# One wait fewer per pair: the gather's half-way wait for the gram, kept in the first block of each pair only

## The chip, the cores and the metric

The kernel runs on 1 core of one Trainium2 chip. The metric is the device time of one execution in microseconds (us); lower is better.

## What is computed

Two residual layers on x of shape 8 x 256 x 128 x 128 (8 images, 256 channels), all in float32. Layer 0 is a modulated deformable sampling; layer 1 is a group whitening whose matrix needs the second moments of the whole result of layer 0.

```
# layer 0
n   = group_norm(x, 32)
off = conv3x3(n, offset_w) + offset_b          # 4 groups, dx and dy
mod = 1 + tanh(conv3x3(n, mod_w) + mod_b)
v   = conv1x1(n, kv_w)[C:] + kv_b              # 8 heads of 32 channels
s   = bilinear sample of v at (pixel + off), times mod
x1  = x + conv1x1(s, out_w) + out_b
# layer 1
n   = group_norm(x1, 32)
cov = per 16 channels, mean over all images and pixels of (n - mu)(n - mu)^T, + 1e-4 I
out = x1 + cov^(-1/2) (n - mu) * weight + bias
```

## The kernel before, in words

Every image has 128 rows of pixels. A **block** is 4 rows (512 pixels) and a **pair** is two blocks, j = 0 and j = 1; an image has 16 pairs, i = 0 to 15. The images run through a software pipeline: while image g is sampled (bilinear sums, output convolution, residual, gram), image a = g + 1 goes through its convolution and its places and weights are computed, and image a + 1 is read for its norm statistics. The last image is sampled with no other image's convolution beside it. Each engine has an instruction list of its own, in an order written out by hand, and the engines meet on semaphores only.

One block of the sampled image takes these steps.

- **GpSimd** (`gather`, L1021): 16 indirect DMAs (L1034), NJ = 16, each fetching 128 patches of 256 floats from the stored `v2` into `patch[n]`. Four patch buffers stand in a ring (RING = 4), n = 2 * (i mod 2) + j. Before its first DMA the gather waits until block (i - 2, j) has been sampled, since that used the same buffer (L1024), and for j = 0 until the places of pair i exist (L1026). Before its ninth DMA (t == NH = 8) it waits for `psG_full[j]` (L1032): the gram of block (i - 3, j) must be finished. The gather runs more than a pair ahead of the sampling. No data of the gather depend on the gram.
- **VectorE** (`sample`, L696): four products and sums for each of two halves (L711 to L730), with the last step of the first part of a block waiting until ScalarE has copied the sample buffer's earlier use out (`psT_free`, L729). Between the two halves it takes the first two convolution rows out of PSUM (`conv_out`, L591 to L603), after them the other two; then places and weights (L622 to L689, once per pair, j = 1) and `residual` (L738).
- **TensorE** (`image`, L1208), per block: two convolution rows (L1143), the transposes of the block three before (`turn_x1`, L1189), the output convolution of the block two before (L1175), two convolution rows, the transposes of the samples of the block before (`turn_samples`, L1165), and the gram of the block three before (`gram_block`, L1203), whose last matmul raises `psG_full[j]`.
- **ScalarE**: copies the transposed samples out (`samples_out`, L1339) and the transposed x1 (`x1_out`, L1357), doubles the convolution rows (L1322) and issues the stores of v (L1330) and of x1 (L1346).

So within one block work goes several times from TensorE to ScalarE or VectorE and back, each time over a semaphore that a matmul raises. With the blocks counted as slots, the gram of block (i - 3, 0) lies in TensorE's slot (i - 2, 1), and that of (i - 3, 1) in slot (i - 1, 0). `psG_full` starts at GRAM_FULL = 3, so that the half-way wait is met from the beginning for the first three pairs of image 0.

`alone(eng)` (L215) adds one to a semaphore that nobody waits for; it keeps a wait on an instruction of its own.

Of the kernel before, what the change touches and what calls it, by code (L numbers as in the profile page):

```python
# [24 lines left out]
PAIRS = BLOCKS // 2  # L25
# [8 lines left out]
NH = NJ // 2  # L34
# [3 lines left out]
GRAM_FULL = 3  # L38
# [31 lines left out]
def deform_zca_kernel(nc, B, x, wA, biasA, bias_off, wO, bias_o, w_z, bias_z, out):  # L70
# [10 lines left out]
    with ctx:  # L81
# [6 lines left out]
        def sem(name):  # L88
            return ctx.enter_context(nc.semaphore(name))
# [97 lines left out]
        psG_full = [sem(f"psG_full{j}") for j in range(2)]  # L187
# [27 lines left out]
        def alone(eng):  # L215


            eng.sem_inc(passed, 1)
# [751 lines left out]
        @block.gpsimd  # L970
        def _(eng):

            for free in (st_used, *row_full[0], *row_full[1], *psO_free,
                         *psO_full, psG_free, *psA_free, psI_free, v_dup):
                eng.sem_inc(free, 1)
            for free in (*sampled[0], *sampled[1]):
                eng.sem_inc(free, 2)
            for free in psT_free:
                eng.sem_inc(free, SAMP_FREE)
            eng.sem_inc(y_add, Y_FREE)  # L980
            for gram_end in psG_full:
                eng.sem_inc(gram_end, GRAM_FULL)
            eng.memset(ident[:, :], 0.0).then_inc(zeros, 1)
            eng.memset(shift[:, :, :], 0.0).then_inc(zeros, 1)
            eng.memset(avg8[:, :], 1.0 / GN1).then_inc(zeros, 1)
            eng.memset(same16[:, :], 1.0).then_inc(zeros, 1)
            eng.wait_ge(zeros, 4)
            eng.affine_select(out=ident[:, :], in_=ident[:, :], compare_op=ALU.not_equal, fill=1.0,
                              base=0, pattern=[[-1, P]], channel_multiplier=1).then_inc(consts, 1)
            for d in range(3):  # L990
                eng.affine_select(out=shift[:, d, :], in_=shift[:, d, :], compare_op=ALU.not_equal,
                                  fill=1.0, base=1 - d, pattern=[[-1, P]],
                                  channel_multiplier=1).then_inc(consts, 1)
            done = 4
            for m, g in ((avg8, GN1), (same16, GZ)):

                eng.affine_select(out=m[:, :], in_=m[:, :], compare_op=ALU.is_ge, fill=0.0, base=0,
                                  pattern=[[-g, P // g], [0, g]],
                                  channel_multiplier=1).then_inc(consts, 1)
                done += 1  # L1000
                eng.wait_ge(consts, done)
                eng.affine_select(out=m[:, :], in_=m[:, :], compare_op=ALU.is_ge, fill=0.0,
                                  base=g - 1, pattern=[[g, P // g], [0, g]],
                                  channel_multiplier=-1).then_inc(consts, 1)
                done += 1

            eng.iota(grid[:, :, 0:G], pattern=[[0, H], [0, G]], base=0, channel_multiplier=1,
                     allow_small_or_imprecise_dtypes=True).then_inc(consts, 1)
            eng.iota(grid[:, :, G:2 * G], pattern=[[1, H], [0, G]], base=0, channel_multiplier=0,
                     allow_small_or_imprecise_dtypes=True).then_inc(consts, 1)  # L1010

            eng.iota(first_patch[:, :, :], pattern=[[0, QR], [1, G]], base=G, channel_multiplier=0,
                     allow_small_or_imprecise_dtypes=True).then_inc(consts, 1)

            eng.memset(taps[:, 0, 0, :], 0.0).then_inc(blanks, 1)
            eng.memset(x1T[:, :, :, :], 1.0).then_inc(blanks, 1)
            eng.memset(gram[:, :, :, :], 0.0).then_inc(blanks, 1)
            eng.memset(vring[0][:, QR, :, 0, :], 0.0).then_inc(blanks, 1)
            eng.memset(vring[1][:, QR, :, 0, :], 0.0).then_inc(blanks, 1)

            def gather(b, k, i, m, j):  # L1021

                n = 2 * m + j
                eng.wait_ge(sampled[j][1], b * PAIRS + i + 1)  # L1024
                if j == 0:
                    eng.wait_ge(placed, b * NQ + i + 1)  # L1026
                alone(eng)
                for t in range(NJ):
                    at = (i * 2 + j) * NJ + t
                    if t == NH:  # L1030

                        eng.wait_ge(psG_full[j], b * PAIRS + i + GRAM_FULL - 2)  # L1032
                        alone(eng)
                    eng.indirect_dma_start(  # L1034
                        out=patch[n][:, t, :], out_offset=None, in_=v2_flat[k],
                        in_offset=bass.IndirectOffsetOnAxis(ap=index[:, at:at + 1], axis=1),
                    ).then_inc(got[n][t // NH], 16)

            with eng.Fori(0, B // 2) as h:
                for k in range(2):  # L1040
                    b = h * 2 + k
                    for j in range(2):
                        eng.wait_ge(v_st[j], (b + 1) * (PAIRS // 2 * 32) + 16)
                    alone(eng)
                    for i in range(PAIRS):
                        for j in range(2):
                            gather(b, k, i, i % 2, j)
# [419 lines left out]
```

## Time and profile before

| | us |
|---|---|
| median of 3 runs | 7104.03 |
| the runs | 7098.11 to 7108.95 |
| the profiled execution | 7085.46 |
| its span, first to last instruction | 7083.2 |
| gathers, first to last DMA issued by GpSimd | 245.4 to 6391.5 |
| granted TensorE clock, mean | 0.813 |

The span falls into three parts: the statistics of image 0 and the first convolutions up to 245 us, the eight sampled images (245 to about 6400 us), and the whitening, which is a matrix iteration and a last pass over all of x1 (to 7083 us). The gathers lie in the middle part only.

How to read the rows below: a row of the timeline has the start in us, the duration in us, engine, line, operation, out<-in with shapes, the number of instructions merged, and in brackets the idle time of the engine before it with what ended it. "remote" stands for a semaphore's rise that comes long after the instruction which raises it, so that the profile doesn't pair the two; "issue" for no wait that shows.

### The profile page before, as it was taken

To read this page: it belongs to the slowest core of one execution; us is meant where nothing else is said; L and a number is where in the kernel's file an instruction comes from. 1 tells how busy PE (TensorE), PEld (TensorE's weight loads), DVE (VectorE), ACT (ScalarE), POOL (GpSimd) and SP (SyncE) were. 2 spreads that over 40 slices of the span, in tenths; PEclk is the share of its full clock that TensorE was granted. 3 is DMA by queue.
4 is the path that set the end of the run, shared out by engine and by line. 5 is a ranking of instruction groups with operands and counts; after the bars stand their busy time and mean duration, and the time that the engine had idled before them with its cause. 6 is when DMAs were issued, how large, how long until landed. Compare 5 with 4: busy or idle time off the path is not lost.

```text
span 7083.2 us, 64542 instructions
## 1 busy us (share of the span) xinstructions
PE 4495.2 (63%) x16382; PEld 2720.3 (38%) x16382; DVE 4889.2 (69%) x12986; ACT 963.0 (14%) x1820; POOL 3900.5 (55%) x4120
## 2 busy tenths in 40 slices
PE   6466656666666656665676656665766634347975
PEld 4234434444334434443443434443444422224432
DVE  7677777777777767776777767776776755556754
ACT  1111111111111111111111111111111100010000
POOL 0366665666666656666666656665666666660000
PEclk9788878888888778877878878887888866678998
DMA  7767666676666657766666656665666644446999
GB/s 254 231 225 227 226 221 205 219 230 215 214 227 221 218 186 233 230 218 224 210 221 229 218 196 224 218 228 178 209 208 202 204 146 138 139 139 240 427 427 415
DMA packets 898773, 1600.84 MB, mean 226 GB/s; under 512 B 82864, under 2 KB 607792, under 8 KB 864816
## 3 DMA queue, kind: packets, MB, share of 16 engines
q0 software_dynamic: 196608, 537.13, 23.7%
q10 hardware_dynamic: 583472, 537.74, 22.3%
q1 hardware_dynamic: 118528, 524.32, 20.7%
q14 instruction: 129, 1.06, 0.0%
q8 instruction: 36, 0.59, 0.0%
HBM read 1061.99 MB, written 536.87 MB: 226 GB/s over the span
## 4 chain that ended last, share of the span: by engine, by line
DVE 49%; another core or an unknown queue 19%; issue 17%; PE 6%; DMA 5%; ACT 2%; DVEq 1%; ACTq 1%; SPq 0%
DVE patch L711 10%; DVE psI L726 5%; DVE psI L724 5%; DVE psI L720 4%; DVE vring L591 4%; DVE samp_mem L730 3%; DVE xr_mem L738 3%; DVE taps L603 2%; DVE bst L514 2%; DMA out_dram<-patch 1%; ACT sampT L1339 1%; DVE weight L684 1%; DVE p_wy L677 1%; PE psA L1143 1%
## 5 line engine op out<-in xcount | busy, mean ns | idle before, releaser
L1034 POOL DMA_INDIRECT patch<-v,index x4096 | 3891.2, 950 | 2488.9 <-issue 1473.6
L1143 PE MATMUL psA<-wB,xa_mem 128*128 128x364 f32 x3664 | 1400.3, 523 | 484.1 <-issue 266.8
L1175 PE MATMUL psO<-sampT,wO_sb 128*128 128x512 f32 x2048 | 1247.6, 762 | 79.3 <-issue 76.1
L1189 PE MATMUL psT<-ident,xr_mem 128*128 128x128 f32 x2048 | 440.9, 370 | 1290.1 <-DVE xr_mem L738 470.6
L1143 PEld LDWEIGHTS psA<-wB,xa_mem 128*128 128x128 f32 x3664 | 727.7, 209 | 1022.1 <-issue 505.6
L711 DVE TENSOR_TENSOR patch<-patch,psI 128x384 f32<-128x384 f32 x2048 | 1035.6, 547 | 52.3 <-issue 16.6
L1189 PEld LDWEIGHTS psT<-ident,xr_mem 128*128 128x128 f32 x2048 | 326.1, 190 | 1454.0 <-issue 873.9
L1175 PEld LDWEIGHTS psO<-sampT,wO_sb 128*128 128x128 f32 x2048 | 505.5, 260 | 652.3 <-issue 648.9
L591 DVE TENSOR_TENSOR vring<-psA,biasB 128x256 f32<-128x256 f32 x956 | 398.5, 417 | 424.3 <-remote 361.9
L730 DVE TENSOR_TENSOR samp_mem<-patch,psI 128x256 f32<-128x256 f32 x1024 | 430.5, 420 | 353.5 <-ACT sampT L1339 186.2
L1203 PE MATMUL psG<-x1T 128*128 128x129 f32 x4096 | 542.4, 288 | 143.0 <-issue 73.9
L1322 ACT ACTIVATE vring<-vring 128x512 f32<-128x512 f32 x512 | 320.8, 627 | 2269.4 <-DVE vring L591 1277.3
L738 DVE SCALAR_TENSOR_TENSOR xr_mem<-psO,bo_sb,xr_mem 128x512 f32<-128x512 f32 x512 | 361.0, 745 | 335.2 <-remote 224.8
L724 DVE TENSOR_TENSOR psI<-patch,psI 128x256 f32<-128x256 f32 x1024 | 439.0, 429 | 213.3 <-remote 136.1
L1203 PEld LDWEIGHTS psG<-x1T 128*128 128x128 f32 x4096 | 508.7, 202 | 167.5 <-issue 131.9
L1339 ACT ACTIVATE sampT<-psT 128x512 f32<-128x512 f32 x512 | 293.0, 596 | 1512.2 <-remote 1123.7
L726 DVE TENSOR_TENSOR psI<-patch,psI 128x256 f32<-128x256 f32 x1024 | 438.4, 428 | 76.8 <-DVE psI L724 37.6
L720 DVE TENSOR_TENSOR psI<-patch,psI 128x256 f32<-128x256 f32 x1024 | 432.8, 423 | 0.1
L1165 PE MATMUL psT<-ident,samp_mem 128*128 128x128 f32 x2048 | 277.1, 279 | 136.7 <-issue 76.0
L1165 PEld LDWEIGHTS psT<-ident,samp_mem 128*128 128x128 f32 x2048 | 246.4, 145 | 226.2 <-issue 163.1
L1357 ACT ACTIVATE x1T<-psT 128x512 f32<-128x512 f32 x512 | 276.6, 586 | 372.0 <-remote 239.5
L603 DVE TENSOR_TENSOR taps<-psA,biasB 128x108 f32<-128x108 f32 x956 | 248.2, 260 | 0.0
(272 smaller groups left out, 2994.9 us busy)
## 6 DMA issues: line engine op xcount, KB each, us to landing
v<-vring ACTq DMA_DIRECT2D x256, 1024.0 KB
xr_mem<-x_dram SPq DMA_DIRECT2D x130, 1024.0 KB
x<-xr_mem ACTq DMA_DIRECT2D x128, 1024.0 KB
xa_mem<-x_dram SPq DMA_DIRECT2D x125, 1024.0 KB, 7.7
xs_mem<-x_dram SPq DMA_DIRECT2D x103, 1024.0 KB, 13.0
patch<-v,index POOLq DMA_INDIRECT x4096
patch<-x SPq DMA_DIRECT2D x54, 1024.0 KB, 12.0
out_dram<-patch ACTq DMA_DIRECT2D x54, 1024.0 KB, 48.7
```

Of the source, the lines that this page charges most:

```text
L591: eng.tensor_tensor(dst, bank[:, 0:C].rearrange("p (g e) -> p g e", g=G), biasB[:, 0:C].rearrange("p (g e) -> p g e", g=G), ALU.add)\
L711: eng.tensor_tensor(two, two, w4[:, 2 * v:2 * v + 2, 0:3].unsqueeze(3).to_broadcast([P, 2, 3, CG]), ALU.mult)
L720: eng.tensor_tensor(total, part[:, :, 3, :], w4[:, :, 3].unsqueeze(2).to_broadcast([P, NH // 2, CG]), ALU.mult)\
L724: eng.tensor_tensor(total, part[:, :, 2, :], total, ALU.add).then_inc(added[j][h][u][0], 1)
L726: eng.tensor_tensor(total, part[:, :, 1, :], total, ALU.add).then_inc(added[j][h][u][1], 1)
L730: eng.tensor_tensor(half[:, t:t + NH // 2, :], part[:, :, 0, :], total, ALU.add)\
L738: eng.scalar_tensor_tensor(xr[m][j][:, o, :], psO[o][:, :], bo_sb[:, o:o + 1], xr[m][j][:, o, :], ALU.add, ALU.add)\
L1034: eng.indirect_dma_start(out=patch[n][:, t, :], out_offset=None, in_=v2_flat[k], in_offset=bass.IndirectOffsetOnAxis(ap=index[:, at:at + 1 ...
L1143: mm = eng.matmul(conv_bank[wide][r][:, 0:NA], row, wB[:, c, :], start=(c == 0), stop=(c == CC - 1))
L1175: mm = eng.matmul(psO[o][:, :], wO_sb[:, h, o * P:(o + 1) * P], sampT[:, h, :], start=(h == 0), stop=(h == CC - 1))
L1189: mm = eng.transpose(psT[h][:, at:at + P], xr[m][j][:, c, row * W:(row + 1) * W], ident[:, :])
L1203: mm = eng.matmul(psG[:, c * (P + 1):(c + 1) * (P + 1)], x1T[:, r, c, 0:P], x1T[:, r, c, :], start=(opens and c == 0 and r == 0), stop=(cl ...
```

## The change

The wait before the ninth DMA of a gather stays in block j = 0 of every pair and is left out in block j = 1, with the semaphore increment beside it. Nothing else is touched: `psG_full[1]` is still raised by TensorE, and ScalarE, VectorE and SyncE still wait for it where they did.

```
                 for t in range(NJ):
                     at = (i * 2 + j) * NJ + t
-                    if t == NH:
-
-                        eng.wait_ge(psG_full[j], b * PAIRS + i + GRAM_FULL - 2)
+                    if t == NH and j == 0:
+
+                        eng.wait_ge(psG_full[0], b * PAIRS + i + GRAM_FULL - 2)
                         alone(eng)
                     eng.indirect_dma_start(
```

## Rows read from the trace of the kernel before

**Rows 1.** The page: span, and the gathers' line among the costliest groups.
```profile
span 7083.2 us, 64542 instructions
...
L1034 POOL DMA_INDIRECT patch<-v,index x4096 | 3891.2, 950 | 2488.9 <-issue 1473.6
```

**Rows 2.** Timeline of GpSimd, three half-way waits in a row, middle of image 3.
```profile
3012.10 0.95 POOL L1034 DMA_INDIRECT patch<-v,index  x1 [3.82 <-remote]
...
3030.88 0.94 POOL L1034 DMA_INDIRECT patch<-v,index  x1 [0.30 <-issue]
3035.60 0.94 POOL L1034 DMA_INDIRECT patch<-v,index  x1 [3.77 <-remote]
...
3059.20 0.95 POOL L1034 DMA_INDIRECT patch<-v,index  x1 [3.80 <-remote]
```

**Rows 3.** Busy us of each engine in one block and in 28 blocks of image 1.
```profile
3012.10:3035.60 23.50, 15.86 (x61) 9.77 (x60) 17.91 (x45) 3.73 (x7) 15.15 (x16) 0.79 0.75 253
...
1109.00:1768.00 659.00, 433.93 (x1673) 272.66 (x1674) 493.24 (x1348) 104.41 (x200) 425.96 (x449) 0.82 0.69 226
```

**Rows 4.** What ended the gathers' idle time, 1109 to 1779 us (us in total, times).
```profile
  remote: 100.9, 27
```

**Rows 5.** Timeline of TensorE and ScalarE around the wait that ends at 3035.60.
```profile
3021.21 1.04 PE L1165 MATMUL psT<-ident,samp_mem 128*128 128x128 f32 x8
3022.08 1.95 PE L1203 MATMUL psG<-x1T 128*128 128x129 f32 x16
...
3034.65 0.60 ACT L1339 ACTIVATE sampT<-psT 128x512 f32<-128x512 f32 x1 [4.37 <-remote]
```

**Rows 6.** Timeline of the last image: GpSimd, TensorE and ScalarE over 32 DMAs without a stop.
```profile
6083.44 0.94 POOL L1034 DMA_INDIRECT patch<-v,index  x1 [6.18 <-remote]
...
6122.26 0.94 POOL L1034 DMA_INDIRECT patch<-v,index  x1 [0.30 <-issue]
6129.34 0.94 POOL L1034 DMA_INDIRECT patch<-v,index  x1 [6.14 <-remote]
...
6093.91 0.60 PE L1165 MATMUL psT<-ident,samp_mem 128*128 128x128 f32 x4
...
6125.60 0.60 ACT L1339 ACTIVATE sampT<-psT 128x512 f32<-128x512 f32 x1 [29.51 <-remote]
6128.41 0.60 ACT L1339 ACTIVATE sampT<-psT 128x512 f32<-128x512 f32 x1 [2.21 <-remote]
```

**Rows 7.** Timeline of GpSimd, the first 48 DMAs of image 1 and of image 2.
```profile
1026.18 0.95 POOL L1034 DMA_INDIRECT patch<-v,index  x1 [5.77 <-issue]
...
1099.40 0.95 POOL L1034 DMA_INDIRECT patch<-v,index  x1 [23.44 <-PE psG L1203]
...
1109.43 0.95 POOL L1034 DMA_INDIRECT patch<-v,index  x1 [0.30 <-issue]
...
1797.40 0.94 POOL L1034 DMA_INDIRECT patch<-v,index  x1 [6.00 <-issue]
...
1831.91 0.94 POOL L1034 DMA_INDIRECT patch<-v,index  x1 [4.75 <-remote]
...
1860.82 0.95 POOL L1034 DMA_INDIRECT patch<-v,index  x1 [8.94 <-PE psG L1203]
...
1870.84 0.95 POOL L1034 DMA_INDIRECT patch<-v,index  x1 [0.31 <-issue]
```

**Rows 8.** Timeline of VectorE, convolution rows at the start of image 6.
```profile
4920.87 0.42 DVE L591 TENSOR_TENSOR vring<-psA,biasB 128x256 f32<-128x256 f32 x1 [4.37 <-remote]
...
4928.57 0.42 DVE L591 TENSOR_TENSOR vring<-psA,biasB 128x256 f32<-128x256 f32 x1 [7.10 <-remote]
```

**Rows 9.** Timeline of image 6, pair 1: the gathers resume, then the next block j = 1.
```profile
4947.91 0.99 POOL L1034 DMA_INDIRECT patch<-v,index  x1 [20.66 <-PE psG L1203]
...
4970.43 0.60 ACT L1339 ACTIVATE sampT<-psT 128x512 f32<-128x512 f32 x1 [4.91 <-remote]
...
4974.11 0.42 DVE L591 TENSOR_TENSOR vring<-psA,biasB 128x256 f32<-128x256 f32 x1
...
4981.69 1.95 PE L1203 MATMUL psG<-x1T 128*128 128x129 f32 x16
```

## The prediction

> **What bounds the kernel now.** I read the page first: the gathers are GpSimd's only long group, 4096 DMAs of 950 ns each, with 2488.9 us of idle before them [rows 1]. By these figures GpSimd is half idle. Its timeline says otherwise: from the resume at 3012.10 to the DMA at 3030.88 there are 15 steps in 18.78 us, 1.252 us from start to start, and after 16 DMAs comes a stop of 3.77 to 3.82 us [rows 2]. A block takes 16 x 1.252 - 0.30 + 3.8 = 23.5 us, and that is what lies between two resumes (3012.10, 3035.60, 3059.20), 47.1 us for a pair. The table by stage shows that no other engine fills it: VectorE is busy for 17.91 of the 23.50 us of one block, TensorE for 15.86, and over 659 us VectorE for 493.24 (75%) [rows 3]. So GpSimd paces the eight images: 20.0 us of issuing and one stop per block. The summary of idle times counts 27 such stops, 100.9 us, in 670 us [rows 4].
>
> The Trainium skill, in "Perfetto Trace Analysis", section "GPSIMD Engine Instruction", says that a GpSimd instruction's reported duration can't be relied on and that the spacing of starts should be used. By durations 32 DMAs would be 30.4 us, by spacing 40.1; 16 spacings and a stop add up to the 23.5 us above, so the trace agrees. (The sum below takes 1.252 us from rows 2 in any case.)
>
> **What the stop is.** It ends on the semaphore that the gram raises, but the gram is not late: its last matmul ended at 3024.03, before GpSimd stopped (31.82), and GpSimd went on only at 3035.60 [rows 2, 5]. In the same way ScalarE got the second half of the samples at 3034.65, though the transposes ended at 3022.25 [rows 5]. So what TensorE raises does not arrive while GpSimd issues; it arrives some 3 us after GpSimd stops. I call this the hold. In the rows it begins about 9 us after a resume (3012.10 to 3021.2). The half-way wait is therefore two things: 3.5 us lost per block, and the only opening in which TensorE can hand work on.
>
> **The change, part by part.**
>
> Removed: the wait and its increment in j = 1; both are run by GpSimd's sequencer while earlier DMAs are under way, so the instructions themselves are worth nothing. The eight DMAs behind the wait, and all gathers queued after them, move ahead by one stop: 3.8 - 0.30 = 3.5 us per pair if nothing takes its place. GpSimd now issues 32 DMAs, 40.1 us, between two stops: the second half of (i, 0), all of (i, 1), the first half of (i + 1, 0).
>
> The waits at a gather's start don't stop it: the buffer's block (i - 2, j) is sampled by the time (GpSimd shows only the 0.30 us there now, [rows 7] at 1109.43, and the next start comes no more than 3.5 us earlier). The DMAs of other queues don't hold it either: the DMA engines are busy 75% of this block [rows 3]. Who waits for the gathers is VectorE, and with a lead of a pair it gains nothing from their coming earlier.
>
> Added: nothing in code, but the hold gets longer. The last image shows 32 DMAs without a stop, since there the gram is early enough: GpSimd runs from 6083.44 to 6123.20, and ScalarE waits 29.51 us for sample transposes of which the first four ended at 6094.51. The hand-offs arrive at 6125.60 and 6128.41, GpSimd resumes at 6129.34 [rows 6]. So after 32 DMAs the hold ends up to 5.2 us after the last DMA, not 3. That image loses little by it, having no convolution beside it.
>
> The other images have to fit two blocks into one opening. The best pattern for the new pair is image 6, pair 1, where GpSimd resumes at 4947.91 just after a gram of a block j = 1 (as it always will) [rows 9]. Block j = 0 then still gets through; its sample transposes fall into the hold, and ScalarE gets them only at 4970.43, after the j = 1 stop [rows 9]. That stop is what is removed. VectorE then stands before the samples' last step (L730), TensorE before its next transposes, until the hold ends. What is late next is the gram of block (i - 2, 1)'s slot, for which the remaining wait asks. From the hand-off at 4970.43 to that gram's end at 4983.64 it took 13.2 us [rows 9], and from a gram's end to GpSimd's resume takes 0.8 us.
>
> So the stop becomes 5.2 + 13.2 + 0.8 = 19.2 us and the pair 40.06 - 0.30 + 19.2 = 59.0 us: +11.9. That supposes that nothing passes in the hold. A little does: at the start of image 6 convolution rows reach VectorE after idle times of 4.37 and 7.10 us [rows 8], where they would follow each other closely. If some three hand-offs pass, the stretch up to 4974.11 is done before the hold ends, 3.7 us less: +8.2. The rows of two image starts weigh the same thing whole: image 1 issues its first 40 DMAs without a stop and needs 1109.43 - 1026.18 = 83.25 us for 48; image 2 has one stop more (4.75 us, after 24) and needs 1870.84 - 1797.40 = 73.44 [rows 7]. A stop that is missing costs 9.8 us net. I take **+10 per pair**, between the ends and nearest to the whole measurement.
>
> Pairs: in image 0 the wait is met for i = 0 to 2, 13 pairs have the stop in j = 1; in images 1 to 6 it is mostly met or short in the first pair, 15 each, 90. Together 103. The last image already runs mostly with one stop in two blocks; by 45.9 us between its two resumes [rows 6] it changes by under 1 us a pair, which I leave out. 103 x 10 = 1030 us. Profiled execution: 7085.5 + 1030 = 8115. The median stands 18.6 us above the profiled time, so I predict **8134 us**. The ends give 7104 + 103 x 8.2 = 7949 and 7104 + 103 x 11.9 = 8330.
>
> **The rivals.**
>
> *The opening isn't needed twice* (faster, 0.09): the hand-offs of two blocks fit into one stop, as in the last image, and the pair takes its 45.9 us. Then 103 x 1.2 = 124 us are saved: 6980. For it: VectorE and TensorE have 25% and more to spare [rows 3]. Against it: the last image has no convolution, and the starts of images 1 and 2 show the reverse. It decides where the gram of the slot j = 1 ends before GpSimd stops; in rows 9 it ends 12 us after the removed stop.
>
> *The waiting itself is the hold* (faster, 0.04): the hold begins about eight DMAs before the stop, which is when a sequencer that runs eight instructions ahead comes to the wait. Without the wait there would be none in j = 1, and 103 x 3.5 = 360 us would go: 6744. Against it: in rows 6 the wait on the way was met and the hold was there all the same. The Trainium skill, "Advanced Engine Details and Errata", section "Engine Queue Depths", gives GpSimd a queue of 8; no run here shows the depth by itself.
>
> *Another wait takes the stop's place* (same, 0.05): GpSimd stops at a gather's start for block (i - 2, j) instead, with an opening there, and the pair stays at 47.1: 7104. Against it: those starts show no idle time now.
>
> *More passes in the hold than I take* (slower, 0.14): a pair pays 2 to 8 us, 7310 to 7930.
>
> *Block j = 0 is caught too* (slower, 0.13): VectorE's 36 us per pair don't fit round a hold of 36 us (40.1 + 5.2 - 9), and the pair pays 13 to 16 us, 8440 to 8750.
>
> **How the numbers follow.** My forecast, 7930 to 8440, has 0.55; with the rivals this is 0.13 faster, 0.05 same, 0.82 slower, by 0.2% (14 us, about what a measurement can tell from no change). For 8 in 10 the range takes in the milder case and all but the end of the worse one: 7300 to 8700, leaving out 0.18 for the first three rivals and about 0.02 at the upper end.
>
> **What would show it.** Right: GpSimd's timeline in images 1 to 6 has one stop per 32 DMAs, of 16 to 20 us, ended by the gram itself and not by "remote"; a pair takes 55 to 59 us; ScalarE's L1339 waits over 20 us once a pair; the granted clock falls below the 0.82 of now [rows 3], since TensorE stands still longer. Wrong: stops of about 6 us (first rival) or 3.8 (second), stops at the gathers' starts (third). The sum would fail first at the 13.2 us, if the new rhythm leaves another share of the block to be done after the hold.

## The result

The kernel after takes **8286.8 us** (median of 4 runs, 8279.6 to 8293.4), the kernel before 7101.1 (4 runs, 7081.4 to 7109.0): ratio **1.1675**, 95% interval 1.1651 to 1.1699. The forecast was 8134, slower. The profiled execution of after took 8280.6 us.

The page of the kernel after, its span and two lines of the costliest groups (busy us, mean ns of one | idle time before them):

```profile
span 8278.9 us, 64414 instructions
...
L1034 POOL DMA_INDIRECT patch<-v,index x4096 | 3893.4, 951 | 3675.9 <-PE psG L1203 1930.7
...
L730 DVE TENSOR_TENSOR samp_mem<-patch,psI 128x256 f32<-128x256 f32 x1024 | 430.5, 420 | 1142.6 <-ACT sampT L1339 894.4
```

One DMA of the gathers still takes 951 ns (950 in [rows 1]); the idle time before them grew from 2488.9 to 3675.9 us, 1187 of the 1196 us that the span grew. What ended that idle time (us in total, times):

```profile
  PE psG L1203: 1930.7, 112
  issue: 1673.5, 3978
  DVE samp_mem L730: 59.3, 4
  remote: 12.4, 2
```

In [rows 4] the stops ended on "remote", a semaphore that came long after its matmul. Now 112 stops end on the gram itself, 17.2 us each: GpSimd waits for a matmul that really runs late. One pair of image 1 in the timeline, from one resume of GpSimd to the next (start, duration, engine, line; in brackets the idle time before):

```profile
1408.44 0.95 POOL L1034 DMA_INDIRECT patch<-v,index  x1 [16.17 <-PE psG L1203]
...
1421.22 1.04 PE L1165 MATMUL psT<-ident,samp_mem 128*128 128x128 f32 x8
1422.09 1.95 PE L1203 MATMUL psG<-x1T 128*128 128x129 f32 x16
...
1431.68 0.42 DVE L591 TENSOR_TENSOR vring<-psA,biasB 128x256 f32<-128x256 f32 x1 [5.56 <-remote]
...
1432.14 0.63 ACT L1322 ACTIVATE vring<-vring 128x512 f32<-128x512 f32 x1 [11.25 <-issue]
...
1438.68 0.43 DVE L724 TENSOR_TENSOR psI<-patch,psI 128x256 f32<-128x256 f32 x1 [2.76 <-remote]
...
1442.88 0.60 ACT L1339 ACTIVATE sampT<-psT 128x512 f32<-128x512 f32 x1 [10.11 <-remote]
...
1447.28 0.95 POOL L1034 DMA_INDIRECT patch<-v,index  x1 [0.31 <-issue]
...
1451.98 0.60 ACT L1339 ACTIVATE sampT<-psT 128x512 f32<-128x512 f32 x1 [8.51 <-remote]
...
1452.61 0.42 DVE L730 TENSOR_TENSOR samp_mem<-patch,psI 128x256 f32<-128x256 f32 x1 [12.09 <-ACT sampT L1339]
...
1463.57 2.05 PE L1203 MATMUL psG<-x1T 128*128 128x129 f32 x16 [0.54 <-DVE gram L747]
...
1466.43 0.95 POOL L1034 DMA_INDIRECT patch<-v,index  x1 [18.21 <-PE psG L1203]
```

GpSimd issues 32 DMAs from 1408.44 to 1448.23. The transposes of the samples end at 1422.26, but ScalarE gets their halves at 1442.88 and 1451.98, the second one 3.75 us after GpSimd has stopped. VectorE's last product step (L730) stands 12.09 us for that. Only then does the next block run through, and its gram ends at 1465.62; 0.8 us later GpSimd goes on. The pair takes 57.99 us instead of 47.1.

A window over almost all of image 1 (busy us of PE, PEld, DVE, ACT, POOL, then granted clock, DMA share and GB/s):

```profile
1268.00:2020.00 752.00, 408.20 (x1530) 243.54 (x1530) 451.05 (x1236) 93.42 (x181) 394.94 (x417) 0.73 0.57 183
```

VectorE fell from 75% [rows 3] to 60%, TensorE from 66% to 54%, the granted TensorE clock from 0.82 to 0.73: nothing fills the time, all wait in turn.

**Where the 1196 us are.** All gaps between the gathers' DMAs in GpSimd's timeline, summed by place (the issuing itself is 623 us per image in both kernels):

| | before, us | after, us | difference |
|---|---|---|---|
| half-way stops, image 0 | 102.6 | 219.1 | +116.5 |
| half-way stops, images 1 to 6 | 776.7 | 1702.2 | +925.5 |
| half-way stops, last image | 115.3 | 132.5 | +17.2 |
| stop before an image's first DMA (7) | 53.1 | 162.8 | +109.7 |
| starts of all other gathers | 115.4 | 133.7 | +18.3 |
| issuing, and all after the last DMA | | | +8 |

So 1041.9 us lie in the 103 pairs of images 0 to 6, 10.1 each. The largest row that the forecast did not have is the fourth. The start of image 2 in the timeline of after:

```profile
2077.55 0.95 POOL L1034 DMA_INDIRECT patch<-v,index  x1 [0.30 <-issue]
...
2095.25 0.63 ACT L1322 ACTIVATE vring<-vring 128x512 f32<-128x512 f32 x1 [6.23 <-DVE vring L591]
2095.91 0.38 ACTq L1330 DMA_DIRECT2D v<-vring  x1
...
2102.03 0.95 POOL L1034 DMA_INDIRECT patch<-v,index  x1 [23.53 <-issue]
```

An image's first gather must wait until all of its v is stored (L1043). The last rows of v are convolution rows of the same hold, the last store goes out 17.4 us after GpSimd's last DMA, and GpSimd stands for 23.53 us where it stood for 6.00 in [rows 7].

### The profile page after: what moved, and what is told of

Read it like the earlier page. It is cut to its first block, busy times and chain, and to the rows that moved or that the text cites. A ratio compares the mean times of both kernels' runs of the same rounds, so it can differ in the third digit from the quotient of the medians.

```text
span 8278.9 us, 64414 instructions
## 1 busy us (share of the span) xinstructions
PE 4540.5 (55%) x16382; PEld 2678.6 (32%) x16382; DVE 4874.5 (59%) x12986; ACT 955.3 (12%) x1820; POOL 3902.6 (47%) x4120
## 3 DMA queue, kind: packets, MB, share of 16 engines
q0 software_dynamic: 196608, 537.13, 20.4%
## 4 chain that ended last, share of the span: by engine, by line
DVE 37%; another core or an unknown queue 24%; issue 23%; PE 7%; DMA 5%; ACT 2%; DVEq 1%; ACTq 1%; SPq 0%
DVE patch L711 8%; DVE psI L726 4%; DVE psI L724 4%; DVE psI L720 3%; DVE vring L591 3%; DVE samp_mem L730 2%; DVE xr_mem L738 2%; PE psO L1175 2%; DVE taps L603 2%; PE psA L1143 1%; DVE bst L514 1%; DMA out_dram<-patch 1%; ACT sampT L1339 1%; PE psO L1289 1%
## 5 line engine op out<-in xcount | busy, mean ns | idle before, releaser
L1034 POOL DMA_INDIRECT patch<-v,index x4096 | 3893.4, 951 | 3675.9 <-PE psG L1203 1930.7
L1143 PE MATMUL psA<-wB,xa_mem 128*128 128x364 f32 x3664 | 1470.0, 541 | 852.4 <-issue 626.1
L1175 PE MATMUL psO<-sampT,wO_sb 128*128 128x512 f32 x2048 | 1223.4, 746 | 167.4 <-issue 165.7
L730 DVE TENSOR_TENSOR samp_mem<-patch,psI 128x256 f32<-128x256 f32 x1024 | 430.5, 420 | 1142.6 <-ACT sampT L1339 894.4
L1189 PEld LDWEIGHTS psT<-ident,xr_mem 128*128 128x128 f32 x2048 | 305.4, 182 | 1973.5 <-issue 1352.5
L1175 PEld LDWEIGHTS psO<-sampT,wO_sb 128*128 128x128 f32 x2048 | 487.1, 250 | 751.9 <-issue 749.2
L724 DVE TENSOR_TENSOR psI<-patch,psI 128x256 f32<-128x256 f32 x1024 | 439.0, 429 | 277.1 <-remote 160.0
L1339 ACT ACTIVATE sampT<-psT 128x512 f32<-128x512 f32 x512 | 288.9, 595 | 1830.2 <-remote 1317.0
```

Source lines behind the costliest of these rows:

```text
L724: eng.tensor_tensor(total, part[:, :, 2, :], total, ALU.add).then_inc(added[j][h][u][0], 1)
L730: eng.tensor_tensor(half[:, t:t + NH // 2, :], part[:, :, 0, :], total, ALU.add)\
L1034: eng.indirect_dma_start(out=patch[n][:, t, :], out_offset=None, in_=v2_flat[k], in_offset=bass.IndirectOffsetOnAxis(ap=index[:, at:at + 1 ...
L1143: mm = eng.matmul(conv_bank[wide][r][:, 0:NA], row, wB[:, c, :], start=(c == 0), stop=(c == CC - 1))
L1175: mm = eng.matmul(psO[o][:, :], wO_sb[:, h, o * P:(o + 1) * P], sampT[:, h, :], start=(h == 0), stop=(h == CC - 1))
L1189: mm = eng.transpose(psT[h][:, at:at + P], xr[m][j][:, c, row * W:(row + 1) * W], ident[:, :])
```

## The experiments

Two theories and a reading of the wait were set against each other. **The hold**: while GpSimd issues gathers, semaphores that TensorE raises don't arrive; each stop in the issuing is an opening. **The order**: the wait on the gram of j = 1 keeps GpSimd in step with TensorE, whatever fills it. **The waiting**: GpSimd's sequencer, standing at the wait, is what holds. Line numbers of the variants shift by a few lines. The edits of e1 to e5 and e9 are shown against the kernel after, the others against the kernel before.

| | us | before beside it | ratio (95%) |
|---|---|---|---|
| e3_no_wait | 8581.0 | 7145.1 | 1.200 (1.197 to 1.204) |
| e5_quarter (after, a quarter of the data) | 8310.6 | 7102.5 | 1.170 (1.168 to 1.172) |
| e4_mirror | 8288.0 | 7100.0 | 1.167 (1.162 to 1.172) |
| e7_every_second | 7810.6 | 7145.1 | 1.092 (1.090 to 1.095) |
| e2_own_in_both | 7710.2 | 7145.1 | 1.078 (1.076 to 1.080) |
| e12_shorter_every_eight | 7603.5 | 7091.0 | 1.070 (1.068 to 1.073) |
| e10_long_every_eight | 7309.5 | 7100.0 | 1.030 (1.027 to 1.033) |
| e1_own_in_j1 | 7292.7 | 7145.1 | 1.020 (1.018 to 1.022) |
| e9_wipe_in_j1 | 7126.0 | 7102.5 | 1.003 (1.002 to 1.005) |
| e6_quarter_before | 7115.7 | 7102.5 | 1.001 (1.000 to 1.003) |
| e8_first_pair | 7054.8 | 7102.5 | 0.994 (0.992 to 0.995) |
| e11_short_every_eight | 6865.6 | 7100.0 | 0.967 (0.964 to 0.970) |

### Is it the wait for the gram, or any stop?

**e1_own_in_j1** gives block j = 1 a stop again, but one that knows nothing of TensorE: GpSimd waits until its own first eight DMAs have landed.

```diff
+                    if t == NH and j == 1:
+                        eng.wait_ge(got[n][0], (b * (PAIRS // 2) + i // 2) * (NH * 16) + NH * 16)
+                        alone(eng)
```

> The changed kernel, but in block j = 1 GpSimd waits before its ninth DMA until its own first eight DMAs have landed; it asks for no gram there. Theory H (what TensorE raises doesn't arrive while GpSimd issues, so each block needs a stop of some 3 us, whatever ends it): the lost time comes back for the most part; a stop of 2 to 4 us per 16 DMAs, a pair of 47 to 49 us, 7100 to 7400 us, and the stops in j = 0 fall from 16 to 20 us to about 4. Rival G (the order matters: GpSimd must not run ahead of the gram of j = 1, and a stop by itself does nothing): about 8290 us, with the 16 to 20 us stops in j = 0 as they are.

GpSimd's timeline, the stops of two blocks in a row:

```profile
1404.43 0.95 POOL L1037 DMA_INDIRECT patch<-v,index  x1 [3.89 <-remote]
...
1429.32 0.95 POOL L1037 DMA_INDIRECT patch<-v,index  x1 [5.17 <-DMA patch<-v,index]
```

The stops in j = 0 are back at 3.9 us, and the loss falls from 16.7% to 2.0%, without any wait for the gram in j = 1. The order is not needed. What is left of the loss lies in the stops themselves: in images 1 to 6 those of j = 1 sum to 443 us against 347 before, since the landing mostly comes later than the gram's semaphore did (4.9 and 3.7 us in the median), and those of j = 0 to 524 against 429, mostly at the start of an image, where the landing takes only 2.5 us and the next stop is a long one.

**e9_wipe_in_j1** goes one step further: at this place GpSimd waits for no other engine, it only does other work, two memsets of the half buffer that the next DMAs fill.

```diff
+                    if t == NH and j == 1:
+                        for r in range(2):
+                            eng.memset(patch[n][:, NH:NJ, :], 0.0).then_inc(wiped, 1)
+                            eng.wait_ge(wiped, (b * PAIRS + i) * 2 + r + 1)
+                            alone(eng)
```

> The kernel after, with two GpSimd memsets of 128 x 2048 floats (1.82 us each, from the row of the memset of gram) on the half of the patch buffer that the next eight DMAs fill, in j = 1 before its ninth DMA. GpSimd waits there for no other engine and is busy all the time, but issues no DMA for about 3.9 us. If the hold is made by GpSimd's issuing of DMAs, TensorE's hand-offs pass during the memsets: the stops in j = 0 go from about 18 us back to about 4, and the time is about that of the variant with the own-landing wait, 7200 to 7400 us. If any work of GpSimd holds, or if the waiting is what lets the semaphores pass, nothing passes: stops in j = 0 of 18 us and more, 8290 to 8700 us.

One pair: GpSimd, then TensorE's transposes of the samples and ScalarE's second half of them:

```profile
1434.46 1.82 POOL L1037 MEMSET patch<- 128x2048 f32 x1
1436.43 1.81 POOL L1037 MEMSET patch<- 128x2048 f32 x1 [0.15 <-issue]
1439.05 0.95 POOL L1040 DMA_INDIRECT patch<-v,index  x1 [0.81 <-POOL patch L1037]
...
1462.55 0.94 POOL L1040 DMA_INDIRECT patch<-v,index  x1 [3.81 <-remote]
...
1423.29 1.04 PE L1171 MATMUL psT<-ident,samp_mem 128*128 128x128 f32 x8
...
1437.23 0.60 ACT L1345 ACTIVATE sampT<-psT 128x512 f32<-128x512 f32 x1 [7.46 <-remote]
```

7126 us: practically the whole loss is undone. The pause is 4.6 us (1434.46 to 1439.05), the next stop 3.81. ScalarE gets the second half at 1437.23, 12.9 us after the transposes ended (1424.33) and while GpSimd's second memset runs. So what opens is neither the gram nor waiting nor an idle GpSimd: it is that GpSimd issues no DMA for a few us.

**e3_no_wait** takes the half-way wait out of both blocks.

```diff
-                    if t == NH and j == 0:
-
-                        eng.wait_ge(psG_full[0], b * PAIRS + i + GRAM_FULL - 2)
-                        alone(eng)
```

> No half-way wait in either block. Theory H: GpSimd issues until the buffer of two pairs before is not yet sampled and stops there; runs of 32 to 48 DMAs, stops of 15 to 30 us at the gathers' starts ended by VectorE's sampling, a pair no faster than in the changed kernel: 8200 to 8800 us. Rival W (what holds the hand-offs back is GpSimd's sequencer standing in a wait for TensorE's semaphore): with no such wait nothing is held, VectorE and TensorE keep up with 40 us of issuing per pair, 6500 to 6800 us.

GpSimd's timeline, two stops in a row:

```profile
1595.19 0.94 POOL L1030 DMA_INDIRECT patch<-v,index  x1 [18.13 <-DVE samp_mem L730]
...
1655.17 0.94 POOL L1030 DMA_INDIRECT patch<-v,index  x1 [20.30 <-DVE samp_mem L730]
```

Slower still, and again about one stop of 18 to 21 us per 32 DMAs, now at a gather's start, where the buffer is not free. If standing at the wait for TensorE's semaphore were the hold, this kernel, which has no such wait, would have been the fastest. It falls.

### Does the block matter, and does the cost add up?

**e4_mirror** keeps the wait in j = 1 and leaves it out in j = 0.

```diff
-                    if t == NH and j == 0:
+                    if t == NH and j == 1:
-                        eng.wait_ge(psG_full[0], b * PAIRS + i + GRAM_FULL - 2)
+                        eng.wait_ge(psG_full[1], b * PAIRS + i + GRAM_FULL - 2)
```

> The mirror of the change: the half-way wait for the gram stays in j = 1 and is left out in j = 0. If a missing stop costs by itself, whichever block it is in, the time is like that of the kernel after, 8200 to 8400 us, with stops of about 18 us, now in j = 1. If the cost comes from the special place of block j = 1 (the places and weights, which VectorE computes there), it is nearer to before: 7100 to 7700 us.

```profile
1445.35 0.94 POOL L1034 DMA_INDIRECT patch<-v,index  x1 [16.19 <-PE psG L1203]
```

8288 us, the time of the kernel after. The block makes no difference; the number of DMAs between two stops does.

**e7_every_second** is the kernel before with the wait in j = 1 left out in every second pair.

```diff
-                    if t == NH:
+                    if t == NH and (j == 0 or i % 2 == 0):
```

> The kernel before, with the wait in block j = 1 left out in every second pair only (i odd). Of the 103 stops that the change removed, 7 in image 0 and 8 each in images 1 to 6 go, 55. If a missing stop has a price of its own (10 to 11 us), 7101 + 55 x 10.5 = 7680 us. If the loss needs the rhythm of one stop per pair throughout, much less: 7100 to 7350.

GpSimd's timeline, three stops in a row, the one at 1471.86 being the first after a missing one:

```profile
1411.72 0.94 POOL L1034 DMA_INDIRECT patch<-v,index  x1 [4.07 <-remote]
...
1471.86 0.94 POOL L1034 DMA_INDIRECT patch<-v,index  x1 [20.43 <-PE psG L1203]
...
1495.75 0.95 POOL L1034 DMA_INDIRECT patch<-v,index  x1 [4.19 <-remote]
```

A missing stop costs at once and leaves nothing behind: the next stop is long, the one after it is normal. The gaps of GpSimd's timeline, summed as in the table above, give 568 us more in the half-way stops of images 0 to 6 for 55 missing ones, 10.3 us each, the unit of the kernel after (10.1). The seven image starts grew here too, by 128 us in all, since the last pair of an image is one of those without the stop; that, and the kernel before, which took 7145 us beside this run and not 7101, is why the time lies above the expected 7680. In e1, where that pair has a stop, they stayed at 4.1 to 10.1 us.

### Is it the traffic?

**e5_quarter** and **e6_quarter_before** are the kernels after and before with gathers that fetch 64 of the 256 floats of a patch.

```diff
-                        out=patch[n][:, t, :], out_offset=None, in_=v2_flat[k],
+                        out=patch[n][:, t, 0:CG], out_offset=None, in_=v2_flat[k],
```

> The kernel after; every gather fetches only the first 64 of the 256 floats of a patch, so three quarters of the gathered data are left out; number of DMAs, of their descriptors and all waits are the same. If the hold comes from GpSimd's issuing (a cost per DMA or descriptor), its stops stay at 14 to 20 us and the time within 3% of 8287 us. If it comes from the gathers' traffic (75% busy DMA engines), the semaphores arrive in time and it comes down to 7000 to 7400 us.

> The kernel before with the same quarter of the gathered data. If the hold comes from issuing, the half-way stops stay at 3.8 us each and the time within 2% of 7101 us. If from the traffic, the semaphores have arrived before the stop, the stops go to 0.3 us, and about 3.5 us x 230 = 800 us are saved: about 6300 us.

The gathers' DMA queue in the page of e5_quarter (packets, MB, share of the engines), a stop of its GpSimd, and one of e6_quarter_before:

```profile
q0 software_dynamic: 131072, 134.48, 7.0%
```

```profile
1591.12 0.94 POOL L1034 DMA_INDIRECT patch<-v,index  x1 [17.97 <-PE psG L1203]
```

```profile
3006.13 0.94 POOL L1034 DMA_INDIRECT patch<-v,index  x1 [4.01 <-remote]
```

A quarter of the bytes (134.48 MB; 537.13 in the kernel before), and both the times (8311 and 7116 us) and the stops stay. The amount of data is not the cause. Each DMA still fetches 128 patches; that number was not varied, so whether it is the issuing itself or something per descriptor or packet (131072 packets remain of 196608) is open.

### How long must a stop be?

**e2_own_in_both** waits in both blocks for the own first eight DMAs, and for no gram.

```diff
-                    if t == NH and j == 0:
-
-                        eng.wait_ge(psG_full[0], b * PAIRS + i + GRAM_FULL - 2)
+                    if t == NH:
+                        eng.wait_ge(got[n][0], (b * (PAIRS // 2) + i // 2) * (NH * 16) + NH * 16)
```

> No wait for a gram at all; in both blocks GpSimd waits before its ninth DMA until its own first eight have landed. Theory H: as with both gram waits or a little better, since the stop ends with the landing and not with a late hand-off: a stop of 2 to 4 us per 16 DMAs, 6900 to 7300 us. If a stop of 2 us is too short for the hand-offs to arrive, they wait for the next stop and the gathers stop at their starts: 7300 to 7700. Rival G: slower than the changed kernel, over 8290 us, since no gram paces the gathers.

```profile
1281.84 0.94 POOL L1033 DMA_INDIRECT patch<-v,index  x1 [2.50 <-DMA patch<-v,index]
...
1300.52 0.94 POOL L1033 DMA_INDIRECT patch<-v,index  x1 [8.98 <-DVE samp_mem L730]
1314.52 0.94 POOL L1033 DMA_INDIRECT patch<-v,index  x1 [4.34 <-DMA patch<-v,index]
```

The landing takes 2.5 us in many blocks and 3.3 us on average (images 1 to 6). That is too short: after every three blocks or so a gather's start stands, here for 8.98 us, until the block that used the buffer before has been sampled. (The Trainium skill, "Perfetto Trace Analysis", section "DMA Instruction — SWDGE (GPSIMD)", says that the reported end of such a DMA is that of its descriptors, not of its data. The trace agrees: the data of the last of the eight come 2.5 us and more after its row ends.)

Three kernels then put a pause ahead of every eight DMAs, one memset of the slots that the DMAs fill afterwards, and have no half-way wait. They differ in its size: NH = 8 slots of 256 floats (e10), NH // 2 (e11), NH // 4 (e12).

```diff
+                    if t % NH == 0:
+                        eng.memset(patch[n][:, t:t + NH // 2, :], 0.0).then_inc(wiped, 1)
+                        eng.wait_ge(wiped, ((b * PAIRS + i) * 2 + j) * 2 + t // NH + 1)
+                        alone(eng)
```

> The same with memsets of 128 x 2048 floats, about 2.4 us without an issue after every eight DMAs: own pace 4 x (9.7 + 2.4) = 48.4 us a pair, 1.3 more than before. If what the issuing fills drains in proportion, TensorE's hand-offs pass twice a block and GpSimd paces: 7150 to 7300 us. If 3 us are needed, long stops at the gathers' starts come in part of the pairs, as with the own-landing wait in both blocks: 7500 to 8300 us.

> No half-way wait at all; instead one memset of 128 x 1024 floats on GpSimd ahead of the first and of the ninth DMA of every gather, so about 1.5 us without an issue after every eight DMAs. GpSimd's own pace would be 4 x (9.7 + 1.5) = 44.8 us a pair, against 47.1 before. If issuing fills something in about 9 us that drains again as soon as GpSimd stops, eight DMAs just fill it and the hold never becomes long: 6750 to 7000 us. If a stop must be 3 us long before anything passes, however short the run of DMAs ahead of it, nothing passes in 1.5 us and stops of 15 us and more come at the gathers' starts, as in the variant without a wait: 8000 to 8600 us.

> Memsets of 128 x 512 floats ahead of the first and ninth DMA of every gather, about 1.35 us without an issue after every eight DMAs; GpSimd's own pace 4 x (9.7 + 1.35) = 44.2 us a pair, against 45.9 with the 1024-float memsets (1.78 us), whose semaphores still came up to 14 us late in places. If some passing in each pause is enough, as there, the pair follows the pace: about 1.7 us x 125 = 210 us below 6866, so 6620 to 6720. If there is a least pause near 1.5 us, below which what is filled by eight DMAs no longer drains, the hold grows together and stops of 15 us and more come back at the gathers' starts: 7500 to 8600 us.

GpSimd's timeline, the pauses of e10, then of e11, then of e12:

```profile
1404.70 1.82 POOL L1032 MEMSET patch<- 128x2048 f32 x1
1407.33 0.95 POOL L1035 DMA_INDIRECT patch<-v,index  x1 [0.81 <-POOL patch L1032]
```

```profile
1419.38 0.97 POOL L1032 MEMSET patch<- 128x1024 f32 x1
1421.16 0.95 POOL L1035 DMA_INDIRECT patch<-v,index  x1 [0.81 <-POOL patch L1032]
```

```profile
1417.46 0.54 POOL L1032 MEMSET patch<- 128x512 f32 x1
1418.81 0.95 POOL L1035 DMA_INDIRECT patch<-v,index  x1 [0.81 <-issue]
...
1459.82 0.53 POOL L1032 MEMSET patch<- 128x512 f32 x1 [9.01 <-DVE samp_mem L731]
```

And ScalarE's group that copies the transposed samples, in the same order, with what ended its idle time:

```profile
L1340 ACT ACTIVATE sampT<-psT 128x512 f32<-128x512 f32 x512 | 278.4, 594 | 234.0 <-PE psT L1166 126.9 <-issue 77.1 <-ACT vring L1323 14.2
```

```profile
L1340 ACT ACTIVATE sampT<-psT 128x512 f32<-128x512 f32 x512 | 285.0, 595 | 354.0 <-remote 163.9 <-PE psT L1166 108.1 <-ACT vring L1323 35.2
```

```profile
L1340 ACT ACTIVATE sampT<-psT 128x512 f32<-128x512 f32 x512 | 289.1, 595 | 913.2 <-remote 730.6 <-issue 94.8 <-PE psT L1166 43.5
```

With pauses of 2.63 us (1404.70 to 1407.33) the late semaphores are gone from ScalarE's first causes, but the pauses cost more than they give back: a pair takes 49.9 us (798.2 us per image, by 16). With 1.78 us many semaphores still come late (163.9 us of this group's idle time), without harm: GpSimd meets no stop at all in the images, not even at their starts (1.8 us there), the pair takes 46.4 us (742.7 us per image, by 16), and the kernel is at **6866 us, 3.3% below the kernel before**. With 1.35 us (1417.46 to 1418.81) the hold grows together again (730.6 us late, stops of 9 us at gather starts, 20 to 24 us at image starts). The least pause after every eight DMAs that keeps this kernel going lies between 1.35 and 1.78 us. Neither of the two expected simple laws holds: it need not be 3 us, and it doesn't shrink at will.

**e8_first_pair** uses the pause once per image, in the kernel before, where the first pair of an image has no stop in j = 1 or a short one. Image 1 issues 40 DMAs without a stop [rows 7]. The expectation below says the same of images 3, 5 and 6; they do stop after 24 DMAs, for 1.88, 2.59 and 3.32 us, but the next stop is a long one all the same (23.50, 22.83 and 20.66 us). Image 3 in the kernel before:

```profile
2592.33 0.95 POOL L1034 DMA_INDIRECT patch<-v,index  x1 [1.88 <-remote]
...
2635.55 0.94 POOL L1034 DMA_INDIRECT patch<-v,index  x1 [23.50 <-PE psG L1203]
```

Images 2 and 4 stop there for 4.75 and 4.77 us, and then for 8.94 and 8.93.

```diff
+                    if t == NH and i == 0 and j == 1:
+                        for r in range(2):
+                            eng.memset(patch[n][:, NH:NJ, :], 0.0).then_inc(wiped, 1)
+                            eng.wait_ge(wiped, b * 2 + r + 1)
+                            alone(eng)
```

> The kernel before with the same two memsets in the first pair of every image only, j = 1, before the ninth DMA, where images 1, 3, 5 and 6 issue 40 DMAs without a stop and then stop for 23.4 us. If a missing stop costs what the variant with every second stop left out showed (12.1 us), four images gain 8 to 12 us each less the added 3.9 us counted in that already, and the two that have a stop there lose up to 3: about 30 us less than before (-0.4%), between -50 and 0. If the long first stop belongs to the start of an image (late places, late rows) and not to the missing stop, it stays, and eight times 3.9 us are added: about +30 us.

GpSimd's timeline at the start of image 1:

```profile
1062.44 1.82 POOL L1033 MEMSET patch<- 128x2048 f32 x1
...
1067.12 0.95 POOL L1040 DMA_INDIRECT patch<-v,index  x1 [0.90 <-POOL patch L1033]
...
1094.81 0.95 POOL L1040 DMA_INDIRECT patch<-v,index  x1 [7.84 <-PE psG L1209]
```

The stop of 23.44 us [rows 7] is 7.84 now, against 4.4 us of added pause. The kernel gains 48 us (0.65%, interval 0.53 to 0.77). The long stop belonged to the one that was missing or too short, not to the start of an image. Runs in which the length of the stop after 24 DMAs is set and doesn't itself hang on the gram say the same of images 1 to 6: 2.5 to 2.6 us in e1 leave 23.7 to 27.6 us for the next stop, 4.6 us in e9 leave 6.0 to 12.7.

## Why the prediction came out as it did

**The mechanism held.** That a hold lies on TensorE's semaphores while GpSimd issues, that the removed wait was an opening, and that the remaining wait would then stand for a gram that really is late: the releasers in the page of after and the timelines of e1 and e9 show each. The signs it named came: one stop per 32 DMAs, ended by the gram (112 of them, most of 16 to 20 us), pairs of 54 to 60 us (most of 55 to 59), a clock below 0.82.

**The pair.** Taken were +10 us, measured are +10.1. The three pieces of the stop were forecast as 5.2 + 13.2 + 0.8 us; the pair shown above has 3.75 + 13.64 + 0.81 = 18.2. So the hold's end after 32 DMAs was too long by 1.5 us, since the rows of the last image gave only an upper bound for it [rows 6]. It made no difference to the sum, because +10 came from the comparison of two image starts [rows 7]. That this hit to 0.1 us is in part luck: neither start has the rhythm of a normal pair. Image 1 stops after 40 DMAs, for 5.2 us longer than the 18.2 of the pair shown, and image 2's two stops, 4.75 and 8.94 us, are 6.1 us longer than two normal ones of 3.8; the two nearly cancel.

**The terms that failed** are two places that the sum left out. The first DMA of an image was covered only by "the waits at a gather's start don't stop it", which speaks of the buffer and of the places; the wait for the stores of v stood in the rows with 5.77 and 6.00 us [rows 7] and was not asked what it waits for. It waits for convolution rows of the last pair, which are in the hold like all else: +109.7 us. The last image was put at under 1 us a pair; its half-way stops and gather starts took 35 us more, 2.2 a pair. With the 8 us of the table's last row that is 153 us, which is what lies between the forecast and the median; 12 us that the pairs cost above the 1030 are set off by the median, which stands 6 us above the profiled time and not 19.

**A sign that didn't come:** ScalarE's L1339 was to wait over 20 us once a pair. It waits 10.11 and then 8.51 us in the pair shown, and never over 11 in images 1 to 6, because one hand-off got through in the middle of the hold (1442.88). The prediction had allowed for some passing, at the convolution rows; one passes there too, at 1431.68.

**The rivals.** That the opening isn't needed twice is refuted by the result, that the waiting is the hold by e3 and e9. Another wait in its place, at a gather's start, came in e2 (8.98 us in the rows shown) and e3 (18.13 and 20.30) and not at 4 us, and not in images 1 to 6 of the kernel after. More passes in the hold, or a second block caught, were not needed: the pair lies at the forecast itself.

**What the prediction had too simple:** a fixed delay of 3 us from GpSimd's stop to the arrival. With a pause after every eight DMAs, 1.78 us is enough; after 24 DMAs at the start of an image 2.6 us does nearly nothing, and 4.6 us most of it. Nor does everything wait for a stop: in the hold hand-offs come late, but some do come (1431.68, 1442.88).

## What to carry to other kernels

A wait without a data dependency may still carry the kernel: before it is removed, ask what other engines get done while the waiting engine stands, and look at what ends the waits of the others ("remote" beside a matmul long finished is the sign). Where GpSimd issues gathers one after another beside TensorE work that goes back and forth over semaphores, give it short regular pauses of its own, and size them by trial: 1.78 us per eight DMAs gained 3.3% here, 1.35 lost 7%, 2.63 lost 3%. And a cost that sits in every stage has to be followed to the stage's borders as well, where a different wait collects it.

## What the runs showed of the hardware

Semaphores raised by TensorE can arrive 10 us and more late while GpSimd issues indirect DMAs back to back: 12.4 us in the kernel before (3022.25 to 3034.65, [rows 5]), 20.6 us in the kernel after (1422.26 to 1442.88). They arrive while GpSimd runs memsets (e9, 1437.23). The delay doesn't depend on the bytes that the gathers move (e5, e6).

It needs a run of issuing, and a pause of a certain length ends it. After every eight DMAs 1.78 us was enough and 1.35 us not (e11, e12). After 24 DMAs at the start of images 1 to 6, pauses of 0 to 2.6 us left a next stop of 22.8 to 27.6 us, one of 3.3 us left 20.7, and those of 4.6 to 4.8 us left 6.0 to 12.7 (the kernel before, e1, e8, e9). Whether what counts is the pause per issued DMA or its length as such, the runs don't separate.

Other engines' semaphores are touched far less. The traces record rises of semaphores; each is taken here against the end of the last instruction before it that raises the same one, from image 0's first gather to image 6's last, for semaphores that only one engine raises. In the kernel before, TensorE's come 3.4 us late in the median and 44% of them over 5 us; of VectorE's 5% come over 1 us late and none over 3.9; of ScalarE's, few of which are recorded, none is late by more than 0.1 us. In the pair of after shown above, VectorE waits 2.76 us for one of its own (L724). With the pauses of e11 TensorE's still come 3.9 us late in the median, but none over 12.8; with the longer ones of e10 only 4% come over 1 us late. What inside the chip is filled or kept busy by the issuing, and why TensorE suffers most, the runs don't tell.
